# Rebuilding the last stage of a two-layer recurrent block: accumulating DMAs, a bias inside the weights, one divide-and-gate pass

## What is computed

```
x1 = x + s * silu(moe(layernorm(x)))              # first layer: s is a linear attention, moe picks 1 of 8 experts
xn = layernorm(x1)
q, k, v = split(xn @ W_qkv)                       # second layer, blocks of 128 rows
p  = softmax_causal(q @ k.T / 16);  p = p / (sum(p) + 1e-6)
s2 = (p @ v) @ W_out.T + b_out
y  = layernorm(xn over the row, eps) * ln_g + ln_b   # the ffn branch, without its expert part
out = x1 + s2 * silu(y)
```

## Time and profile before

| | |
|---|---|
| median of 3 runs | 606.52 us (604.61 to 607.42) |
| the profiled execution | 606.05 us, of it 604.4 us of span |
| busy in the span | PE 86%, PEld 79%, DVE 85%, ACT 63%, POOL 70% |
| DMA, mean over the span | 112 GB/s |
| TensorE clock granted, mean | 0.971 |

### The profile page before, as it was taken

How to read it: one execution, slowest core, us unless ns; L and a number is a source line. 1 busy time by engine, 2 the same in 40 slices (tenths; PEclk the granted TensorE clock), 3 DMA queues, 4 the chain that set the end, 5 groups by cost and what they waited for, 6 DMA issues and landing times. The chain is left out here.

```text
span 604.4 us, 13496 instructions
## 1 busy us (share of the span) xinstructions
PE 517.7 (86%) x3722; PEld 477.2 (79%) x3723; DVE 511.8 (85%) x1516; ACT 377.9 (63%) x843; POOL 421.4 (70%) x499
## 2 busy tenths in 40 slices
PE   1898999999999997499999659888888888888883
PEld 1888999999999997499999548777777777777772
DVE  5698988888888866777788487999999999999994
ACT  3776877878787873277777426555555555555552
POOL 4478988879787976132220267888888888888773
PEclk9999999999999998799999779999999999999998
DMA  9712222222233112266788541233333333333211
GB/s 235 193 56 74 83 71 80 83 83 69 69 96 97 36 44 71 91 200 211 240 251 271 155 132 53 83 106 107 109 102 104 106 105 106 105 109 102 79 48 58
DMA packets 59397, 67.59 MB, mean 112 GB/s; under 512 B 11864, under 2 KB 53728, under 8 KB 59360
## 3 DMA queue, kind: packets, MB, share of 16 engines
q1 hardware_dynamic: 51488, 45.63, 25.1%
q0 software_dynamic: 7872, 21.51, 12.3%
HBM read 39.85 MB, written 27.26 MB: 111 GB/s over the span
## 5 line engine op out<-in xcount | busy, mean ns | idle before, releaser
L1578 POOL DMA_INDIRECT moe<-expert_rows,gather_u x64 | 69.3, 1083 | 37.8 <-DVE gather_u L1425 22.0
L1388 ACT ACTIVATE xn2nd<-res,shift,rstd 128x256 f32 (+1 forms) x64 | 34.9, 593 | 85.9 <-POOL shift L1589 85.9
L806 POOL DMA_INDIRECT sorted_rows<-xn,row_u x64 | 64.0, 999 | 17.5 <-issue 14.9
L1272 PE MATMUL q_ps<-xt,wqk 128*128 128x256 f32 x256 | 62.4, 388 | 0.7 <-ACT xt L1365 0.7
L887 POOL DMA_DIRECT2D xg<-sorted_rows x36 | 19.7, 548 | 59.8 <-issue 32.8
L1292 PE MATMUL v_ps<-wvo,xt 128*128 128x256 f32 x256 | 61.3, 383 | 0.0
L790 POOL TENSOR_TENSOR xn<-xn 128x512 fp32r<-128x512 f32 x32 | 41.4, 1292 | 25.8 <-ACT xn L425 25.1
L1272 PEld LDWEIGHTS q_ps<-xt,wqk 128*128 128x128 f32 x256 | 49.7, 195 | 7.9 <-ACT xt L1365 1.1
L1283 PE MATMUL t_ps<-ident,xn2nd 128*128 128x128 f32 x128 | 21.8, 295 | 38.9 <-ACT xn2nd L1388 38.9
L1283 PEld LDWEIGHTS t_ps<-ident,xn2nd 128*128 128x128 f32 x128 | 14.4, 146 | 51.0 <-ACT xn2nd L1388 43.7
L1292 PEld LDWEIGHTS v_ps<-wvo,xt 128*128 128x128 f32 x256 | 46.9, 193 | 5.1
(11 more groups left out here) (219 smaller groups left out, 2003.7 us busy)
## 6 DMA issues: line engine op xcount, KB each, us to landing
expert_rows<-y SPq DMA_DIRECT2D x36, 256.0 KB, 2.8
xa<-in_L_attn_x SPq DMA_DIRECT2D x32, 256.0 KB, 2.9
xin<-in_L_attn_x SPq DMA_DIRECT2D x32, 256.0 KB, 3.4
out_rows<-att SPq DMA_DIRECT2D x32, 256.0 KB
xg<-sorted_rows SPq DMA_DIRECT2D x36, 128.0 KB, 2.2
xg<-sorted_rows POOLq DMA_DIRECT2D x36, 128.0 KB, 2.7
wdn<-in_L_ffn_wd SPq DMA_DIRECT2D x2, 512.0 KB, 7.4
sorted_rows<-res SPq DMA_DIRECT2D x8, 128.0 KB, 6.2
```

The source lines that it names most:

```text
L806: nc.gpsimd.indirect_dma_start(out=z.sorted_dram.ap(), out_offset=bass.IndirectOffsetOnAxis(ap=row_u[:, i // CU, k:k + 1], axis=0), in_=xn ...
L1272: m = nc.tensor.matmul(q_ps[:, j, :], wqk[:, k, j * P:(j + 1) * P], xt[:, i % 2, k, :], start=(j == 0 and k == 0), stop=(k == KD - 1), ski ...
L1578: nc.gpsimd.indirect_dma_start(out=moe[:, i, t, :], out_offset=None, in_=z.expert_dram.ap(), in_offset=bass.IndirectOffsetOnAxis(ap=gather ...
```

## The change

Nearly all of it is in the last stage.

- `res` becomes x1 in two steps: DVE multiplies `moe` by `res` into `res` (unit n+5), and POOL issues a DMA that adds x from DRAM into `res` (`add_x`, unit n+4 of POOL's step). The buffer `xin`, its load by SP and the DVE addition go.
- The output is summed in DRAM: SP stores x1 to the output as soon as its statistics are taken, and POOL later issues a DMA that adds the gated rows (`add_out`). POOL's addition of x1 goes.
- Mean and variance come from the aggregating instruction and three small ones; the gate's normalisation is computed from `res` in two DVE passes with `ln_b` inside, so POOL's addition of `ln_b` goes.
- `W_qkv` has its last row subtracted from every row (in the experts stage, by DVE; the sum of a normalised row is zero, so nothing changes). The last element of every normalised row is then free, and is set to a constant one; through it `b_out` enters the value weights. A matmul with `bias_rows` per tile makes up for the 1e-6 in the divisor.
- Division and gating become one pass per tile (`gate_rows`), instead of two passes per tile and one over both.
- The weight loads move from the end of the experts' loop on SP to the front of it, with one more (`w2_end`).
- POOL's step gets a new order: first three waits, then the norm, then `add_x`, `add_out`, and the gathers of unit n+6 last.

```diff
@@ experts, SP @@
             load_first(sp, 0)
+            sp.dma_start(z.w2_end[:], W_qkv[D - 1, :].partition_broadcast(P)).then_inc(g["weights_loaded"], 16)
+            for dst, src in ((z.w2, W_qkv), (z.wo, W_out)):
+                sp.dma_start(dst[:], src.rearrange("(k p) n -> p k n", p=P)).then_inc(g["weights_loaded"], 16)
+            for dst, src in ((z.bout, b_out), (z.lng, ln_g), (z.lnb, ln_b)):
+                sp.dma_start(dst[:], src.partition_broadcast(P)).then_inc(g["weights_loaded"], 16)
             with sp.Fori(0, ROUNDS - 2) as r:
...
@@ experts, DVE @@
             four_pairs(QUAD, second=True)
+            dve.wait_ge(g["weights_loaded"], 16 * 6)
+            nc.vector.tensor_tensor(z.w2[:], z.w2[:], z.w2_end[:].unsqueeze(1).to_broadcast([P, KD, 3 * D]), ALU.subtract).then_inc(g["w2_centred"], 1)
...
@@ second_layer, SP @@
+            def store(n, i):
+                if there(n):
+                    sp.wait_ge(g["stats_done"], UT * n + UT)
+                    sp.dma_start(out_units[n], tiles(n)).then_inc(x1_stored[i], 16)
+            def step(n, i, _):
+                store(n + 4, at(i, 4))
...
@@ second_layer, PE attend @@
+                    for t in range(UT):
+                        nc.tensor.matmul(a_ps[:, t, :], prt[:, i % 2, t, :], vo[:, i % 2, t, :], start=(t == 0), stop=False,
+                                         skip_group_check=True)
+                        m = nc.tensor.matmul(a_ps[:, t, :], z.ones_b[:], bias_rows[:], start=False, stop=True, skip_group_check=True)
...
@@ second_layer, DVE @@
+            def scale_rows(n, i):
+                if there(n):
+                    dve.wait_ge(moe_loaded[i % SLOTS], turns(n, i, 16 * UT) + 16 * UT)
+                    nc.vector.tensor_tensor(tiles(n), moe[:, i % SLOTS], tiles(n), ALU.mult).then_inc(g["moe_scaled"], 1)
+            def x1_complete(n, i):
+                if there(n):
+                    dve.wait_ge(x_added[i % SLOTS], turns(n, i, 16) + 16)
...
+            def gate_rows(n, i):
+                if there(n):
+                    dve.wait_ge(g["inv_ready"], n + 1)
+                    dve.wait_ge(g["gate_ready"], n + 1)
+                    dve.wait_ge(g["att_ready"], n + 1)
                     if there(n, SLOTS):
+                        dve.wait_ge(out_added[i % SLOTS], turns(n, i, 16))
+                    for t in range(UT):
+                        m = nc.vector.scalar_tensor_tensor(att[:, i % SLOTS, t, :], a_ps[:, t, :], inv[:, i % SLOTS, t:t + 1], zg[:, i % SLOTS, t, :], ALU.mult, ALU.mult)
+                    m.then_inc(g["gated"], 1)
             def step(n, i, _):
+                back, next_one = (n - 1, at(i, -1)), (n + 1, at(i, 1))
+                scale_rows(n + 5, at(i, 5))
+                x1_complete(n + 3, at(i, 3))
+                if there(n + 8, SLOTS):
+                    index(n + 8, at(i, 8))
+                norm_stats(n + 3, at(i, 3))
+                stats_complete(n + 3, at(i, 3))
+                centre_gate(*next_one)
+                find_moments(n + 3, at(i, 3))
+                gate(*back)
+                prepare_norm(n + 3, at(i, 3))
                 base_divisor(*back)
+                scale_gate(*next_one)
+                maximum(n, i)
                 invert_divisor(*back)
+                gate_rows(*back)
...
@@ second_layer, POOL @@
+            def rows_free(n, i):
+                if there(n):
                     pool.wait_ge(g["index_ready"], n + 1)
+                    if there(n, SLOTS):
+                        pool.wait_ge(g["moe_scaled"], n - SLOTS + 1)
...
+            def rows_scaled(n, i):
+                if there(n):
+                    pool.wait_ge(g["moe_scaled"], n + 1)
+            def add_x(n, i):
+                if there(n):
+                    nc.gpsimd.dma_start(tiles(n), x_units[n], accum_op=ALU.add).then_inc(x_added[i % SLOTS], 16)
...
+            def rows_gated(n, i):
+                if there(n):
+                    pool.wait_ge(x1_stored[i], (n - i) * (16 // TURN) + 16)
+                    pool.wait_ge(g["gated"], n + 1)
+            def add_out(n, i):
+                if there(n):
+                    nc.gpsimd.dma_start(out_units[n], att[:, i % SLOTS], accum_op=ALU.add).then_inc(out_added[i % SLOTS], 16)
             def step(n, i, _):
+                rows_free(n + 6, at(i, 6))
+                rows_gated(n - 2, at(i, -2))
+                rows_scaled(n + 4, at(i, 4))
                 norm_scale(n + 2, at(i, 2))
+                add_x(n + 4, at(i, 4))
+                add_out(n - 2, at(i, -2))
+                gather(n + 6, at(i, 6))
```

More of the change, by code:

```diff
@@ L47, in sb @@
             return whole.enter_context(nc.sbuf_tensor(name, shape, dt))
+        z.scattered, z.moe_loaded, z.x_added, z.out_added = (
+            [whole.enter_context(nc.semaphore(f"{name}{i}")) for i in range(count)]
+            for name, count in (("scattered", 8), ("moe_loaded", 4), ("x_added", 4), ("out_added", 4)))
         z.wq = sb("wq", [P, 2, z.KD, z.D], F32R)
@@ L96, in scope, with pipeline @@
     return sb, ps, sems
-def pipeline(eng, first, step, last, units, slots):
+def pipeline(eng, first, step, last, units, slots, tail=1):
     for n in range(first, slots):
         step(n, n % slots, n // slots)
-    with eng.Fori(1, units // slots - 1) as r:
+    with eng.Fori(1, units // slots - tail) as r:
         for i in range(slots):
             step(r * slots + i, i, r)
-    for n in range(units - slots, last + 1):
+    for n in range(units - tail * slots, last + 1):
         step(n, n % slots, n // slots)
@@ new lines, in centre_gate, with scale_gate @@
+            def centre_gate(n, i):
+                if there(n):
+                    dve.wait_ge(g["shift_ready"], n + 1)
+                    for t in range(UT):
+                        nc.vector.scalar_tensor_tensor(zg[:, i % SLOTS, t, :].unsqueeze(1), one_tile(n, t), neg_mean[:, i % SLOTS, t:t + 1], lng_half[:].unsqueeze(1),
+                                                       ALU.add, ALU.mult).then_inc(g["z_based"], 1)
+            def scale_gate(n, i):
+                if there(n):
+                    for t in range(UT):
+                        dve.wait_ge(g["z_based"], UT * n + t + 1)
+                        nc.vector.scalar_tensor_tensor(zg[:, i % SLOTS, t, :], zg[:, i % SLOTS, t, :], rstd[:, i % SLOTS, 1, t:t + 1], lnb_half[:],
+                                                       ALU.mult, ALU.add).then_inc(g["z_ready"], 1)
@@ L1528, in gate_rows @@
             def gate_rows(n, i):
                 if there(n):
-                    dve.wait_ge(g["att_scaled"], UT * n + UT)
+                    dve.wait_ge(g["inv_ready"], n + 1)
                     dve.wait_ge(g["gate_ready"], n + 1)
-                    nc.vector.tensor_tensor(att[:, i], att[:, i], zg[:, i], ALU.mult).then_inc(g["gated"], 1)
-            def step(n, i, _):
-                back, next_one, ahead = (n - 1, at(i, -1)), (n + 2, at(i, 2)), (n + 3, at(i, 3))
-                begin = isinstance(n, int) and n == -2
-                if not begin:
-                    scale_rows(*ahead)
-                inverse_variance(*next_one)
-                base_divisor(*back)
-                normal_variance(*next_one)
-                gate(*back)
-                normal_variance_eps(*next_one)
-                if begin:
-                    scale_rows(*ahead)
-                add_rows(*ahead)
-                invert_divisor(*back)
-                scale_gate(n + 1, at(i, 1))
-                norm_stats(*ahead)
-                maximum(n, i)
-                meet_halves(*ahead)
-                attend(*back, 0)
-                square_difference(*ahead)
-                attend(*back, 1)
-                variance(*ahead)
```

231 lines of the change are left out of this document (87 added, 144 removed).

## The result

The changed kernel takes 623.28 us (median of 4 runs, 621.9 to 625.4) against 606.33 for the kernel before (604.61 to 607.42, 4 runs): a ratio of 1.0285, 95% interval 1.0243 to 1.0327. It is slower, and lies outside the range. The profiled execution has a span of 620.7 us, 16.3 more than the 604.4 of before.

A forecast was written before the change was run, and what follows sets the result against it. VectorE bounds the last stage; afterwards a two-step ring through POOL would, at 7.1 us against 7.51. Steady -9.8, filling +6.1, loop end -2.0, last steps -1.8, experts stage +2: -5.5 from 606.05 gives 600.5 us, range 587 to 622.

The forecast's parts named there:

- VectorE's step: Last stage: VectorE's work per step falls from 7.5 to 5.55 us (D), as 1.7 us of blocking by POOL's additions disappears.
- Rival D: Last stage: VectorE keeps 0.7 us of blocking, period 7.45 us, 609 us; chance 0.14 together with the band around no change.
- The ring: Last stage: VectorE's end, POOL's whole step, gather landing and VectorE's next step form a two-step chain; period 7.1 us.
- POOL's part of the ring: Last stage: from VectorE's step end through norm, two accumulating issues and gathers to `scale_rows`, 8.65 us.
- rival A: Last stage: gathers land late behind accumulating DMAs (4.9 us), or issues take 1.7 us; period 7.7, 615 us; chance 0.24.
- POOL's work: Last stage: norm, two accumulating issues and gathers sum to 6.15 us of POOL work a step, under TensorE's.
- PE: Last stage: TensorE's work was put at 6.6 us a step, including 0.3 for two more matmuls.
- Filling: Start of the last stage: `add_x` delays the gathers behind it, so VectorE's step 3 begins later, +6.1 us.
- Experts stage: Stage before the last: early weight loads and the centring pass cost +2 us, bounds 0 and 5.
- Last write and last steps: End of the last stage: last five steps at TensorE's 6.6 us give -1.8 us; the last write changes by 0.
- Rival C: Last stage: the DMA engines or the landing of `add_x` become the bound; period 8.5 us, 634 us; chance 0.08.
- B: Last stage: cheap issues (0.85) and landing of 3.2 to 3.4 us bring the period to 6.6; 588.5 us; chance 0.18.

## Why the prediction was wrong, step by step

**VectorE's step: right.** 5.47 us against D = 5.55 (its terms add up to 5.53), and the 1.7 us of blocking are gone: `neg_mean`, the slowest of the small operations, lasts 0.38 us once and 0.16 in the next steps. Rival D is out.

**The ring: right as a mechanism.** The bound is where it was put, VectorE waits before `scale_rows` for the gather, released by DMA, and T = (POOL's part + D) / 2 gives the measured period. Taking it apart by order alone gave 21.8 us, though not all of it is the ring's standing still, as said there.

**POOL's part of the ring: the step that failed.** Forecast 8.65 us, measured 10.1:

| term | forecast | measured | from the timeline |
|---|---|---|---|
| handover of `gated` | 0.1 | 0.40 | 481.10 to 481.50 |
| norm, and the loop's gap | 1.35 | 1.80 | to 483.30 |
| two accumulating issues | 2.2 | 2.93 | to 486.23 |
| first gather | 1.3 | 1.41 | to 487.64 |
| second gather until `scale_rows` | 3.7 | 3.56 | to 491.20 |

The largest is the price of an accumulating issue. I took a = 1.1, near the plain direct load of 128 rows; it is 1.47 (2.93 / 2). That lay inside the bounds of 0.85 and 2.0, and I chose the row that was nearest in form but plain and half as large. The runs without accumulation show that it is the accumulation: 1.85 us for both. The rest are the hand-over and the loop's instructions: I had 0.1 us for both, and they are 0.75 us more. The 1.45 us together are more than three times the 0.45 at which rival A decides. Rival A named "the same comes from a = 1.7" beside a late gather. What happened is half of this second form, a = 1.47, and half the hand-over and the gap, which no rival named; the gather that ends the ring came no later than forecast (3.56), though the median over all gathers rose to 4.0 from 3.7. A's 615 us plus the excess of the two terms further down, 5.2 and 2.5, is 622.7, where 623.28 was measured; so near it is partly luck, since the causes are only in part those that A gave.

**POOL's work: too low.** 6.15 us forecast, 7.1 in the changed kernel and 6.93 in the other order with an operation more. It did not bind here, but it lies above the forecast of PE's 6.6, and it bounds what mending the order can bring.

**PE: too high.** 6.6 us forecast; where TensorE is busy all the time a step takes 6.2 to 6.3, no more than the 6.3 of work before.

**Filling: size off.** The first `rstd` was forecast at 357.8 with the stage's first gather at 343.2, 14.6 us after it; it came at 364.79, 14.4 after the first gather at 350.39. So its start was right. The POOL rounds behind it were put at 5.0 us; from one `rstd` to the next they take 5.6 to 5.7 (370.52, 376.08, 381.80), since they carry the same dearer issue: +8.6 instead of +6.1.

**Experts stage: wrong.** Forecast 2 us with bounds 0 to 5, measured 7.2 in the profile and 9.0 by the kernel with the loads late. I had seen that the loads come "to the edge" of the four pairs of slack and then taken a value below the edge. The sixth load goes over it; then the granted clock falls as well, which I had not counted at all. The size of the pass itself was right, 1.76 us against 1.75. The pause was 3.25 us, below the 5 that I had named as the sign, and still the stage lost more than 5: the sign was set too coarse, since the clock and the pass add to it.

**Last write and last steps: right** within 0.9 us each. Rival C did not occur in the changed kernel, no wait for x stands before the statistics; nor did B, for which the ring would have had to be shorter than forecast.

**The rule beside the sum** said that the DMA share would pass 70%. The trace shows 0.69 in the steady stretch, against 0.34. The Trainium skill, "DMA: Bandwidth & Descriptors", section "Rules for kernel authors", states that an accumulating DMA reads its destination. In the bytes that read is not to be seen: HBM read is 40.25 MB with the output accumulated and 40.25 without, and in the steady stretch 134 GB/s are moved against 98, far from double. What the runs show is more time of the DMA engines for the same bytes, 30.5% of 620.7 us against 24.5% of 608.3 us in the POOL queue, in packets of 1 KB that take about twice as long as plain ones of that size.

## What to carry to other kernels

Before taking work off the busiest engine, write down the ring that the new order closes, and put every issue, hand-over and loop instruction of the serial part into it: a wait for the very last result of another engine, placed at the front of a queue whose last instruction feeds that engine, makes all the queue's work serial. An addition done by a DMA isn't free for the engine that issues it: here each took 1.47 us of POOL's ring, where POOL's own addition had lasted 1.27, and leaving the final addition on VectorE with the wait gone was 40 us faster. A load moved into a stage whose DMA engines are 76% busy should be judged by whether a late row can stop TensorE, since a pause can cost clock as well.

## What the runs showed of the hardware

- Accumulating direct DMAs of 256 KB from POOL: the issue lasts 1.34 us (SBUF destination) and 1.79 us (DRAM, right behind the other); plain ones in the same places 0.79 and 0.76. A plain one right behind an accumulating one still lasts 1.30.
- They land after 4.5 and 6.0 us (medians), where the plain forms took 3.4 and 3.8 in the same window, and each takes 256 packets of 1 KB where the plain form takes 64 of 4 KB.
- A packet of 1 KB of an accumulating DMA takes 0.115 us of a DMA engine on the mean, a plain one of 1 KB in SP's queue 0.052.
- An operation that follows a small one across the loop's instructions starts 0.5 us later than without a loop (0.66 against 0.14); over the stage that was worth about 3 us.
- DMA engines at 1.00 for 6 us did not stop TensorE with five loads in flight; with a sixth, broadcast, of 384 KB, they did, for 1.65 to 3.25 us in seven kernels. With pauses of 2.75 to 3.25 us the granted clock went to 0.50 for 3.4 or 6.8 us, in five of the kernels; with 2.32 and 1.65 it stayed at 1.00.
